# A macaron block on one core: first tiles stored from ScalarE, attention's head and second routing rearranged, two ring slots loaded behind the first turned buffers

## What is computed

```python
def _L0_ffn_ref(hidden_states, gate_w, bias, w_gate, w_up, w_down, ws_gate, ws_up, ws_down):
    E, K, H, F = (64, 6, 512, 192)          # 8 groups of 8, of which 4 are kept
    x = hidden_states.reshape(-1, H)
    topk_w, topk_ids = _grouped_topk(x @ gate_w, bias)
    y = _routed_moe(x, topk_w, topk_ids, w_gate, w_up, w_down)     # CAP = 96 tokens an expert
    shared = jax.nn.silu(x @ ws_gate) * (x @ ws_up) @ ws_down
    return (y + shared).reshape(orig_shape)

x = L0_attn_X                                # 4 x 512 x 512
x = x + 0.5 * _L0_ffn_ref(_layernorm(x), ...)
x = x + _L0_attn_ref(_layernorm(x), ...)     # norm with weights, 16 heads of 32, rotary on half, softmax, + input
x = x + 0.5 * _L0_ffn_ref(_layernorm(x), ...)
```

## Time and profile before

| what | us |
|---|---|
| median of three runs (1332.97 to 1335.03) | 1334.72 |
| the profiled execution | 1328.23 |
| its span | 1326.3 |
| PE busy | 1182.2 (89%) |
| DVE busy | 614.6 (46%) |
| ACT busy | 508.0 (38%) |
| POOL busy | 531.5 (40%) |

### The profile page before, as it was taken

How to read it: one execution, slowest core, us unless ns; L and a number is a source line. 1 busy time by engine, 2 the same in 40 slices (tenths; PEclk the granted TensorE clock), 3 DMA queues, 4 the chain that set the end, 5 groups by cost and what they waited for, 6 DMA issues and landing times.

```text
span 1326.3 us, 26369 instructions
## 1 busy us (share of the span) xinstructions
PE 1182.2 (89%) x10288; PEld 773.8 (58%) x10288; DVE 614.6 (46%) x1189; ACT 508.0 (38%) x1300; POOL 531.5 (40%) x418
## 2 busy tenths in 40 slices
PE   7787999999985879999999999999997999999770
PEld 5432877776764656665556565565534777777550
DVE  7394122221224766777866976651692222222120
ACT  2222111121102358888788787772222111121100
POOL 0022455555633374534443443200023565555543
PEclk9998999999997989999999999999898999999995
DMA  9957999999997622433343424230878999999987
GB/s 334 398 174 248 317 322 324 322 318 321 318 289 205 196 74 72 95 83 80 96 101 76 113 68 109 80 124 17 296 259 286 332 323 320 320 319 317 313 216 133
DMA packets 180971, 288.71 MB, mean 218 GB/s; under 512 B 21488, under 2 KB 103792, under 8 KB 180848
## 3 DMA queue, kind: packets, MB, share of 16 engines
q1 hardware_dynamic: 147232, 218.92, 51.4%
q0 software_dynamic: 23808, 57.69, 19.1%
q10 hardware_dynamic: 9808, 10.42, 2.4%
HBM read 210.15 MB, written 55.57 MB: 200 GB/s over the span
## 4 chain that ended last, share of the span: by engine, by line
PE 49%; DVE 9%; ACT 3%; issue 3%; DMA 2%; POOL 1%; DVEq 0%; SPq 0%; ACTq 0%; POOLq 0%
PE ps L380 11%; PE ps L396 7%; PE ps L445 5%; PE ps L488 4%; PE ps L476 4%; PE ps L456 4%; PE ps L502 3%; PE ps L431 2%; PE ps L539 2%; PE ps L363 2%; DVE Mx L1142 2%; ACT ps L756 1%; PE ps L282 1%; DVE keyT L1017 1%; ACT xF L740 1%
## 5 line engine op out<-in xcount | busy, mean ns | idle before, releaser
L380 PE MATMUL ps<-bufT,gu 128*64 128x96 f32 x6144 | 292.7, 256 | 11.5 <-issue 9.2
L380 PEld LDWEIGHTS ps<-bufT,gu 128*64 128x64 f32 x6144 | 282.4, 174 | 20.6 <-issue 11.9
L1142 DVE TENSOR_REDUCE Mx<-ps 128x1 f32<-128x512 f32 x256 | 170.7, 684 | 77.2 <-PE ps L456 76.0
L756 ACT ACTIVATE ps<-ps,Mx 128x512 f32<-128x512 f32 x256 | 174.8, 685 | 49.1 <-DVE Mx L1142 43.0
L396 PE MATMUL ps<-wd,h 64*96 64x512 f32 x768 | 180.4, 602 | 5.0 <-DVE osb L1059 3.2
L711 ACT COPY bufT<-ps 128x384 f32<-128x384 f32 x128 | 60.6, 477 | 316.6 <-PE ps L363 316.6
L769 ACT ACTIVATE PT<-ps 128x512 f32<-128x512 f32 x256 | 158.4, 619 | 50.0 <-PE ps L476 47.9
L1278 POOL DMA_INDIRECT buf<-xn_d,tok x128 | 130.0, 1016 | 102.5 <-issue 58.3
L1049 DVE TENSOR_TENSOR h<-sg,ps 128x288 f32<-128x288 f32 x64 | 29.1, 454 | 303.9 <-PE ps L380 303.9
L1059 DVE TENSOR_SCALAR osb<-ps,gt 96x512 f32<-96x512 f32 x128 | 89.9, 742 | 145.7 <-PE ps L396 145.7
L456 PE MATMUL ps<-St 96*128 96x512 f32 x256 | 119.1, 483 | 8.8 <-ACT ps L756 6.3
(11 more groups left out here) (158 smaller groups left out, 1607.6 us busy)
## 6 DMA issues: line engine op xcount, KB each, us to landing
gu<-in_L_ffn_w_gate SPq DMA_DIRECT2D x128, 384.0 KB, 10.3
gu<-in_L_ffn_w_up SPq DMA_DIRECT2D x128, 384.0 KB, 11.5
wd<-in_L_ffn_w_down SPq DMA_DIRECT2D x192, 256.0 KB, 11.4
St<-HL SPq DMA_DIRECT2D x186, 128.0 KB, 2.3
qkr<-in_L_attn_W_in SPq DMA_DIRECT2D x30, 256.0 KB, 3.4
xn_d<-XN SPq DMA_DIRECT2D x24, 256.0 KB, 4.6
X<-in_L_attn_X SPq DMA_DIRECT2D x4, 1024.0 KB, 11.4
ya_d<-X SPq DMA_DIRECT2D x4, 1024.0 KB, 10.8
```

The lines of the kernel that those rows point to most:

```text
L380: t = e.matmul(bk[64 * k:64 * k + 64, CAP * j:CAP * j + CAP], gu[:, 2 * k + m, c, j:F:3], f.bufT[(2 * q + k) % 4][:, c, :], start=(c == 0) ...
L756: e.activation(bk, bk, ACT.Exp, bias=Mx[:, qt, hl:hl + 1], accum_out=Dn[:, qt, hl:hl + 1]).then_inc(a_den, 1)
L1142: e.tensor_reduce(Mx[:, qt, hl:hl + 1], bank((4, 5, 7)[n % 3]), AX, ALU.max, negate=True).then_inc(a_max, 1)
```

## The change

Eight things change, of which the diff shows the lines.

1. In f1 the 16 normalised tiles are stored by ScalarE, each behind its own copy. SyncE loads ring slots 0 and 1 before X is copied to ya_d, and 2 to 4 behind. VectorE's wait for the last four stores moves behind the fourth counted step.
2. In both mixtures ring slots 6 and 7 wait for the second turned buffer (`f_bT`); in f1 the gate and up part of slot 6 was loaded earlier and stays there.
3. The value weights of attention are fetched behind slot 7 of f1; the weights of units 0 and 1 behind the last ring load, into memory of their own (wq), and halved by ScalarE and VectorE in the last expert steps. Value weights are halved after the last scatter.
4. The iterations -2 and -1 are replaced by a straight head: project units 0 and 1, value 0, the 16 scores of unit 0, value 1, rows. Unit 1's projections go to banks 3 and 6.
5. The first four score tiles (NDIR) are computed from HL by three matmuls of 32 rows each, without the stacked copy.
6. Values 2 and 3 go to iteration 0 in place of fillers; tiles 4 and 5 to iteration 0, 6 and 7 to iteration 1.
7. GpSimd rotates unit 1 and halves the weights of unit 2 before it adds tiles 8 to 15.
8. Between attention and f2 tiles 12 to 15 are turned and multiplied earlier and in another order, the remainder part of the first shared group moves into `pe_route`, and the Sigmoid table is loaded ahead of the last tile's copy.

```diff
         def pe_route(e, f):
-            pe_shared_up(e, f, 0, (2,))
+            pe_shared_up(e, f, 0, (1, 2) if f.n else (2,))
...
         def pe_scores(e, u, j):
             d, hl, qt = St[u % 3], j // 4, j % 4
             n = 16 * u + j
-            if qt == 0:
+            if n < NDIR:
+                e.wait_ge(a_lo, 2)
+            elif qt == 0:
                 e.wait_ge(s_st[u % 3][hl], 48 * (u // 3 + 1))
...
+            if n < NDIR:
+                p = slice(32 * hl, 32 * hl + 32)
+                for m, (x, y) in enumerate(((1, 2), (1, 3), (0, 2))):
+                    t = e.matmul(bank((4, 5, 7)[n % 3]), HL[p, x, 128 * qt:128 * qt + 128], HL[p, y, :], start=(m == 0),
+                                 stop=(m == 2), tile_position=(32 * hl, 0), skip_group_check=True)
+                t.then_inc(a_sc, 1)
+                return
...
-            return (4, 5) if u == -1 else (u + 6,) if 0 <= u and u + 6 < NT else ()
+            return (2 * u + 4, 2 * u + 5) if u < 2 else (u + 6,) if u + 6 < NT else ()
...
-            for u in range(-2, NU + 1):
+            for u in range(2):
+                for k in range(2):
+                    for third in range(3):
+                        pe_project(e, u, k, third)
+            for third in range(3):
+                pe_value(e, 0, third)
+            for j in range(16):
+                pe_scores(e, 0, j)
+                if j % 2:
+                    pe_busy(e, 1)
+            for third in range(3):
+                pe_value(e, 1, third)
+            pe_rows(e, 0)
+            for u in range(NU + 1):
...
             pe_attention(e)
-            pe_shared_up(e, f2, 0, (1,))
-            for i in range(12, NT):
-                if i == 12:
-                    pe_fill(e)
-                    pe_fill(e)
-                    pe_fill(e)
-                pe_tile(e, f2, i)
-                if i > 12:
-                    pe_logits(e, f2, i - 1)
-            pe_logits(e, f2, NT - 1)
+            pe_tile(e, f2, 12)
+            pe_tile(e, f2, 13)
+            pe_logits(e, f2, 12)
+            pe_tile(e, f2, 14)
+            pe_logits(e, f2, 13)
+            pe_fill(e)
+            pe_fill(e)
+            pe_logits(e, f2, 14)
+            pe_tile(e, f2, 15)
+            pe_logits(e, f2, 15)
...
         def act_first_weights(e):
 
+            for u in range(2):
+                e.wait_ge(s_wqk, 64)
+                e.copy(wq[u][:, 0, :, :, :], wqr[u][:, :, :, :]).then_inc(w_hi, 1)
             e.wait_ge(f_d, E)
-            e.wait_ge(s_wqk, 32)
-            e.copy(wqk[:, 0, :, :, :], qk0[:, :, :, :]).then_inc(w_hi, 1)
             e.wait_ge(s_wv, 16)
             e.copy(wv[0][:, :, :], v0[:, :, :]).then_inc(w_hi, 1)
...
+            for k in range(2):
+                act_split(e, 0, k)
+            stack(e, 0, (1, 3))
+            for j in range(16):
+                act_scores(e, 0, j)
+                if j in (10, 13):
+                    act_split(e, 1, (10, 13).index(j))
+            act_log(e, 0)
+            fill(e, 0)
+            for u in range(NU + 1):
...
             for i in range(12, 16):
                 act_tile(e, f1, i)
+                store_xn(e, f1, i)
...
             act_root(e, f2, 1)
-            for i in range(12, 15):
-                act_tile(e, f2, i)
+            act_tile(e, f2, 12)
+            act_tile(e, f2, 13)
             act_root(e, f2, 2)
+            act_tile(e, f2, 14)
+            e.preload_act_table(ACT.Sigmoid)
             act_tile(e, f2, 15)
...
             if not f.n:
                 e.wait_ge(s_c, 32)
-                for i in range(NT - 4, NT):
-                    stored(e, f, i)
...
             e.wait_ge(f_step, 15 * f.n + 4)
+            if not f.n:
+                for i in range(NT - 4, NT):
+                    stored(e, f, i)
...
+            for k in range(2):
+                dve_project(e, 0, k)
+                rotate(e, 0, k)
+            for k in range(2):
+                rest(e, 0, k)
+            dve_value(e, 0)
+            for j in range(16):
+                dve_scores(e, 0, j)
+                if j in (5, 7):
+                    dve_project(e, 1, (5, 7).index(j))
+                if j == 11:
+                    dve_weights(e, 2)
+            dve_lse(e, 0)
+            for i in range(4, 7):
+                dve_stat(e, i)
+            for u in range(NU + 1):
...
         def pool_attention(e):
-            e.wait_ge(w_lo, 2)
             e.memset(St[0][96:98, 1, :, :].bitcast(F32), 1.0).then_inc(a_ones, 1)
             e.wait_ge(a_ones, 1)
-            e.wait_ge(a_xT, 4)
+            e.wait_ge(a_lo, 2)
             for i in range(4, 8):
                 pool_add(e, i)
             e.wait_ge(a_add, 8)
+            for k in range(2):
+                rotate(e, 1, k)
+            for k in range(2):
+                rest(e, 1, k)
+            pool_weights(e, 2)
+            e.wait_ge(w_lo, 4)
             e.memset(St[1][96:98, 1, :, :].bitcast(F32), 1.0).then_inc(a_ones, 1)
             e.wait_ge(a_ones, 2)
-            for u in range(-2, NU + 1):
+            for i in range(8, NT):
+                pool_add(e, i)
+            e.wait_ge(a_add, NT)
+            e.memset(St[2][96:98, 1, :, :].bitcast(F32), 1.0).then_inc(a_ones, 1)
+            e.wait_ge(a_ones, 3)
+            for u in range(NU + 1):
...
             e.wait_ge(f_hs, 4 * f.n + 4)
+            e.wait_ge(f_bT, 64 * f.n + 2)
             if f.n:
                 load_up(e, f, NR - 2)
             load_down(e, f, NR - 2)
             e.wait_ge(f_shc, 16 * f.n + NT)
             load(e, f, NR - 1)
+            if not f.n:
+                value_weights(e)
...
-            e.wait_ge(f_gu, 2 * 24 + 2)
+            e.wait_ge(f_d, 2 * 27 + 2)
             fetch(e, 0)
+            fetch(e, 1)
...
+            load(e, f1, 0)
+            load(e, f1, 1)
             for g in range(4):
-                for i in range(4 * g, 4 * g + 4):
-                    store_xn(e, f1, i)
-                if g < 3:
-                    load(e, f1, g)
                 e.wait_ge(s_x[g], 16)
                 keep(e, f1, g)
+            load(e, f1, 2)
             load(e, f1, 3)
+            e.wait_ge(f_xn, NT)
             e.wait_ge(s_y, 64)
```

More of the change, by code:

```diff
@@ L444, in pe_project @@
                 c, (x, y) = n // 3, parts[n % 3]
-                t = e.matmul(bk, wqk[:, x, c, k, :], xT[y][:, c, :], start=(n == 0), stop=(n == 11))
+                t = e.matmul(bk, w[:, x, c, k, :], xT[y][:, c, :], start=(n == 0), stop=(n == 11))
             if third == 2:
@@ L473, in pe_expo @@
                 e.wait_ge(a_ones, min(u, 2) + 1)
+                if u == 0:
+                    e.wait_ge(a_cos, 4)
             if n >= 2:
@@ L817, in act_attention @@
                         act_log(e, u + 1)
-                    if u == -1 and j == 15:
-                        fill(e, 0)
         def act(e):
@@ L1049, in dve_experts @@
                     e.tensor_tensor(f.h[q % 2][:, :], f.sg[q % 2][:, :], ps[1 + q % 2 * 2][:, 1, 0:3 * CAP], ALU.mult).then_inc(f_h, 1)
+                if q == E // 2 and not f.n:
+                    dve_first_weights(e)
                 if q:
@@ L1349, in pool_attention @@
                         pool_weights(e, u + 3)
-                    if u == -1 and j == 10:
-                        for i in range(8, NT):
-                            pool_add(e, i)
-                        e.wait_ge(a_add, NT)
-                        e.memset(St[2][96:98, 1, :, :].bitcast(F32), 1.0).then_inc(a_ones, 1)
-                        e.wait_ge(a_ones, 3)
                     if u == 1 and j == 15:
@@ L1456, in sp_attention @@
             again(e, 2)
-            for u in range(-2, NU + 1):
+            stack(e, 0, (2, 0))
+            fetch(e, 2)
+            again(e, 3)
+            e.dma_start(wout[:, :, :], W_out.rearrange("(c p) n -> p c n", c=4)).then_inc(s_wo, 16)
+            stack(e, 1)
+            for u in range(NU + 1):
                 for j in range(16):
```

85 lines of the change are left out of this document (38 added, 47 removed).

## The result

The changed kernel takes 1316.64 us (median of 4 runs, 1314.64 to 1323.31) beside 1333.85 for the kernel before (4 runs, 1332.90 to 1335.03): a ratio of 0.988, 95% interval 0.984 to 0.992. On another chip, with more runs, it was 1319.25 beside 1331.98, 0.991 (0.989 to 0.993). So the gain is 13 to 17 us; 16.8 had been forecast as a change, 1318 as a time. The profiled execution took 1314.64 us, its span is 1312.8 (before 1326.3). The medians say 17.2 on this chip and 12.7 on the other.

What follows compares the result with a forecast made beforehand. DMA volume over rate was taken to bound both expert stages, chains the rest. Terms -13.7 + 4.3 - 8.6 + 1.0 - 3.0 + 3.2 = -16.8 us gave a span near 1309.5, forecast 1318 (range 1305 to 1328).

Steps and rivals of the forecast that it cites:

- Part 1: Stores and first routing: stores issued from ScalarE land near 47 us, hidden from VectorE; -13.7 us (-9 to -15).
- Part 2: First expert stage: delayed slot loads (+1.0) and value weights (+3.3) lengthen it; +4.3 us (+1 to +8).
- Scatter chain: End of first expert stage: early weight halving falls on idle engines, scatters end the stage anyway; 0 us (-2 to +2).
- Part 3: Attention's head: 13.1 us shorter, less 4.5 us for ScalarE's late split; -8.6 us (-3 to -14).
- the +4.5 for GpSimd's queue: Attention after the head: ScalarE's split waits for GpSimd's rotation behind additions and memsets; +4.5 us (0 to +9).
- Part 4: Attention's units 0 and 1: values replace fillers at equal length, one more tile each; +1.0 us (0 to +2).
- Part 5: Second routing's head: sigmoid 6.2 us sooner, less 3.65 for the moved shared group; -3.0 us (0 to -6).
- Part 6: Second expert stage: two slots load about 8 us later, losing 1.0 MB of carrying; +3.2 us (0 to +7).
- B: Rival, first routing: ScalarE's stores land no sooner than SyncE's; +4.5 us, 1322 in all; chance 0.12.
- C: Rival, attention's head: GpSimd's order eats the whole gain and the clock drops; +6 us, 1324; chance 0.11.
- D: Rival, both expert stages' ends: no cost, TensorE's 4 us earlier start kept in each; 1306; chance 0.11.
- E: Rival, weight ring in expert stages: each delayed slot costs a full 10.7 us landing period; 1356; chance 0.04.

## Why the prediction was right, and where it wasn't

- **Part 1** (-13.7; measured -14.2): right, by its own mechanism, with a landing 1.6 us later than assumed and no slack left. That the 9.8 us in SyncE's queue were the cause was only a part: SyncE's late issue weighed 7 us.
- **Part 2** (+4.3; +3.6 and +6.4 in the two profiles): mechanism right, its split uncertain. The wait's share was 3.5 by the carrying lost rather than 1.0 (1.3 to 4.3 by the lengths); the values (3.3 forecast) cost 1.2 to 2.6 at the stage's end by the two profiles without the wait, 2.3 to 5.1 by the one with the values late.
- **Scatter chain** (0, -2 to +2; measured -2.4 and -5.3): the failed step is that moving the value weights was counted where they went and not where they came from. For the whole kernel that megabyte is worth the same in either place (1320.17 and 1319.25).
- **Part 3** (-8.6): the head's -13.1 was -10.9, mis-sized because VectorE's work was taken for the chain; the +4.5 for GpSimd's queue was a wait that isn't there.
- **Part 4** (+1.0; +2.7 and +4.3): the failed step. A tile more in a unit isn't its work on an idle engine: in unit 0 it is a root that stands late in VectorE's order (read from rows), in unit 1 a bank that comes free late, and the clock behind it. Parts 3 and 4 together: -7.6 forecast, -3.8 measured.
- **Part 5** (-3.0; +0.3): the sign was wrong. It was assumed that shorter pauses could only help the clock; the clock halved among the small matmuls, and the fillers then ran at it ahead of tile 15. Where the clock stayed, the lists came 3.0 us sooner, as forecast. What makes it fall in one profile and not in the other stays open.
- **Part 6** (+3.2; +5.5, of which about 5 by the carrying lost): mechanism right, mis-sized: 1.6 MB of carrying was lost instead of 1.0.

Of the rivals, B and C fell (small tile at 48.70; the additions cost nothing), D fell by the run without the wait, E by size: a delayed slot costs the transfer time lost, not a landing period.

## What to carry to other kernels

Where the DMA engines are the bound (busy through the whole stage, and an earlier start of the compute buys nothing), a wait put in front of a load costs the carrying lost: the bytes not moved meanwhile over the rate. Don't take a constant product of length and rate for a proof of it; that is only the volume. Before you credit a DMA queue with a late landing, split it into the time until the engine issues and the time from issue to landing. And where work is moved, book it at both places; where small matmuls follow a pause, use real work for a filler and keep fillers away from what is waited for.

## What wasn't expected of the hardware

- The DMA rate of a saturated expert stage varied between executions of the same instructions: in the second stage with the wait it was 313 GB/s in one profile and 308 in the one with the subtraction moved, which is 282.2 or 287.6 us; without the wait 319 and 315, which is 277.1 or 280.4. What sets it stays open.
- A fall of the clock is close to an on-off matter that a remote edit can tip: unit 1 took 31.0 or 29.4 us, and sigmoid 12.8 or 9.6, with the same instructions in the same place. Most profiles agree: 31.0 in nine of ten, and 12.8 in nine of ten. What tips it stays open.
